# An RWKV block with sixteen routed experts: whole slots of 128 rows plus mixed slots of four 32-row pieces

## What is computed

```
x = x + attn(_layernorm(x))          # time mix (r, w, k, v, two scans, Wo), channel mix (Wkey, relu^2, Wval, gate Wrec)
x = x + ffn(_layernorm(x))
# ffn, t = 8192 tokens, 16 experts, top 1
logits = hidden @ router_w.T
top_vals, top_idx = top_k(logits, 1)
scores = sigmoid(...)                                   # zero for all experts but the chosen one
routed_in = hidden[None] * scores.T[:, :, None]
gate, up = split(einsum('nth,nhf->ntf', routed_in, gate_up_proj))      # 128 -> 2 x 128
routed = einsum('ntf,nfh->nth', up * silu(gate), down_proj).sum(0)     # 128 -> 128
shared = silu(hidden @ shared_gate.T) * (hidden @ shared_up.T) @ shared_down.T   # width 512
```

## Time and profile before

| | us |
|---|---|
| median of 3 runs | 490.42 |
| the profiled execution | 490.73 |
| its span, first to last instruction | 488.6 |
| granted TensorE clock, mean | 0.999 |
| PE busy in the span | 477.0 |
| DVE, ACT, POOL busy | 371.1, 323.8, 352.3 |
| transposes of the first two pairs start | 353.0 |
| last down product of a slot, end | 467 |
| last matmul, end | 483.9 |

### The profile page before, as it was taken

The page is one execution under the profiler, slowest core; times in us unless marked ns, Lnnn a source line. Parts: engine busy times, 40 slices in busy tenths (PEclk is TensorE's granted clock), DMA queues, the critical chain, the costliest instruction groups (busy, mean ns, idle before and its releaser), DMA issues.

```text
span 488.6 us, 10463 instructions
## 1 busy us (share of the span) xinstructions
PE 477.0 (98%) x3093; PEld 388.2 (79%) x3093; DVE 371.1 (76%) x1056; ACT 323.8 (66%) x623; POOL 352.3 (72%) x573
## 2 busy tenths in 40 slices
PE   8999999999999999999999999999999999999995
PEld 7655777868777778686777867888899999999995
DVE  7889899899999998997899989747445555555535
ACT  2667887978978879777687886554365555555521
POOL 6655688898888988986788777677236676667750
PEclk9999999999999999999999999999999999999999
DMA  7007001102101011020101101111389854442028
GB/s 238 2 1 281 22 12 56 54 13 66 33 34 65 24 45 54 12 67 21 46 25 41 45 1 44 45 44 37 117 197 225 226 158 136 145 139 76 24 52 294
DMA packets 33031, 39.33 MB, mean 80 GB/s; under 512 B 4913, under 2 KB 29113, under 8 KB 32720
## 3 DMA queue, kind: packets, MB, share of 16 engines
q1 hardware_dynamic: 26640, 24.98, 17.8%
q0 software_dynamic: 5760, 13.16, 7.8%
q10 hardware_dynamic: 576, 0.52, 0.3%
HBM read 21.69 MB, written 17.93 MB: 81 GB/s over the span
## 4 chain that ended last, share of the span: by engine, by line
PE 77%; DVE 6%; issue 5%; POOL 5%; DMA 4%; ACT 2%; SPq 1%; POOLq 0%; DVEq 0%; ACTq 0%
PE bank L427 17%; PE bank L420 9%; PE bank L444 6%; PE bank L414 4%; PE bank L822 3%; PE bank L823 3%; PE bank L815 3%; PE bank L435 3%; PE bank L528 3%; PE bank L514 3%; PE bank L540 3%; PE bank L524 3%; PE bank L519 3%; PE bank L688 2%; PE bank L697 2%
## 5 line engine op out<-in xcount | busy, mean ns | idle before, releaser
L427 PE MATMUL bank<-hT,wm 128*128 128x256 f32 x512 | 124.7, 383 | 0.6 <-ACT kr L908 0.6
L427 PEld LDWEIGHTS bank<-hT,wm 128*128 128x128 f32 x512 | 92.0, 190 | 18.7 <-issue 8.3
L1528 POOL DMA_INDIRECT sorted_rows<-rows,posi x64 | 71.9, 1124 | 19.6 <-issue 16.9
L1612 POOL DMA_INDIRECT out<-shared x55 | 53.2, 967 | 37.3 <-DVE shared L1442 22.3
L420 PEld LDWEIGHTS bank<-wm,k 128*128 128x128 f32 x512 | 61.7, 192 | 7.6 <-issue 6.6
L420 PE MATMUL bank<-wm,k 128*128 128x128 f32 x512 | 62.1, 275 | 0.0
L1084 ACT ACTIVATE er<-bank 128x256 f32<-128x256 f32 x40 | 15.4, 384 | 44.8 <-PE bank L823 44.3
L1450 DVE TENSOR_TENSOR e<-er,bank 128x256 f32<-128x256 f32 x40 | 16.9, 421 | 23.0 <-ACT er L1084 21.1
L444 PE MATMUL bank<-wm,actA 128*128 128x128 f32 x240 | 32.9, 280 | 0.0
L1612 POOL DMA_INDIRECT out<-rows x24 | 23.1, 964 | 11.3 <-DVE rows L1442 5.3
L944 ACT ACTIVATE h<-rows,smE 128x128 f32<-128x128 f32 x64 | 26.3, 482 | 6.7 <-POOL smE L1504 6.7
(11 more groups left out here) (256 smaller groups left out, 1293.9 us busy)
## 6 DMA issues: line engine op xcount, KB each, us to landing
shared<-sorted_rows SPq DMA_DIRECT2D x56, 128.5 KB, 2.9
shared<-x SPq DMA_DIRECT2D x16, 256.0 KB, 3.0
rows<-sorted_rows SPq DMA_DIRECT2D x24, 128.5 KB, 2.5
wexp<-w_exp SPq DMA_DIRECT2D x2, 1536.0 KB, 8.4
sorted_rows<-filler SPq DMA_DIRECT2D x17, 128.5 KB
shared<-out SPq DMA_DIRECT2D x6, 256.0 KB, 4.7
out<-shared SPq DMA_DIRECT2D x12, 128.0 KB, 2.7
sorted_rows<-rows,posi POOLq DMA_INDIRECT x64
```

Of the source, the lines that this page charges most:

```text
L427: ins = mm(dst[:, j * HALF:(j + 1) * HALF], W(name, 2 * pair_ + j), src[:, half * HALF:(half + 1) * HALF], start=True, stop=True)
L1528: g_.indirect_dma_start(sorted_ap, bass.IndirectOffsetOnAxis(posi[t % 3][:, g:g + 1].bitcast(U32), 0), rows[t % 3][:, g, :], None).then_in ...
L1612: g_.indirect_dma_start(out, bass.IndirectOffsetOnAxis(xr[k % RING][:, j, D:D + 1].bitcast(U32), 0), xr[k % RING][:, j, D + 1:ROW], None, ...
```

## The change

The slots are cut in another way. There are now 48 whole slots (`UNI`), always of one expert, and 20 mixed slots of four pieces of 32 rows (`SUBS` = 80 pieces), each piece with an expert of its own: 24 whole pairs and 10 mixed pairs, 34 in all. The pairs 5, 8, 11 and so on to 32 are the mixed ones. For a mixed slot SP issues four loads of 32 rows, ACT copies four sets of weights, and PE makes four gate and four up products with 32 columns of the transposed rows each, and four down products whose stationary operand has 32 columns and whose result goes to 32 partitions. The filler is 32 rows for an expert, and all 16 of its DMAs are issued in one go ahead of pair 5, with a wait for all of them. The ring of weight copies grows to 23, and ACT copies up to four pieces a turn ahead. The tables take 18 steps on DVE and their constants are made ahead of the third tile's `z` step.

```diff
-NS = NTOK // P + NE
-NP = NS // 2
+SUB = P // 4
+UNI = NTOK // P - NE
+SUBS = NTOK // SUB + NE - 4 * UNI
+NS = UNI + SUBS
+MIXED = range(5, 34, 3)
+NP = UNI // 2 + len(MIXED)
...
-        xw = [q, an, xn2T, th, rv]
-        XW = len(xw)
+        xw = q + an + xn2T + th + rv + k2 + a + xa + kr[2:4] + h
...
+        def parts(k):
+            return 4 if k in MIXED else 1
...
+        def copied(m):
+            return min(copies_to(NP - 1), max(copies_to(min(m, NP - 1)), 4 * (m + 1))) if m >= 0 else 0
...
             for k in range(NP):
-                if k in FILL_PAIRS:
-                    sp.dma_start(sorted_ap[bass.ds(tails[k - FILL_PAIRS[0]], P), :], filler[:, :]).then_inc(s["fill_out"], 16)
-                if k == FULL_SLOTS // 2:
+                if k == MIXED[0]:
+                    tails = entries(SP_ENGINE, tail_i, 0, FILL_ROW - P, NE)
+                    for row in tails:
+                        sp.dma_start(sorted_ap[bass.ds(row, SUB), :], filler[0:SUB, :]).then_inc(s["fill_out"], 16)
                     sp.wait_ge(s["fill_out"], 16 * (NE + 1))
                 for j in range(2):
-                    sp.dma_start(xr[k % RING][:, j, :], sorted_ap[bass.ds(first_rows[at_ + j], P), :]).then_inc(
-                        s[loaded(k)[0]], 16)
+                    if k in MIXED:
+                        for c in range(4):
+                            sp.dma_start(xr[k % RING][c * SUB:(c + 1) * SUB, j, :],
+                                         sorted_ap[bass.ds(sub_rows[entry(k, j, c) % LOADED], SUB), :]).then_inc(s[loaded(k)[0]], 16)
...
-                    for j in stores(k):
-                        ins = mm(grp(XDN_B[k % 2], j), grp(xact[k % 4], j), w_of(k, j, 2), start=True, stop=True)
+                    for j in range(2):
+                        for c in range(parts(k)):
+                            rows_ = slice(c * SUB, (c + 1) * SUB) if k in MIXED else slice(0, P)
+                            ins = mm(grp(XDN_B[k % 2], j)[rows_, :], grp(xact[k % 4], j)[:, rows_], w_of(k, j, c, 2),
+                                     start=True, stop=True)
-                    for j in stores(k):
-                        mm(grp(XGU_B[k % 2], j), w_of(k, j, 0), xhT(k, j), start=True, stop=True)
-                        ins = mm(grp(XGU_B[k % 2], 2 + j), w_of(k, j, 1), xhT(k, j), start=True, stop=True)
+                    for j in range(2):
+                        for c in range(parts(k)):
+                            rows_ = slice(c * SUB, (c + 1) * SUB) if k in MIXED else slice(0, P)
+                            mm(grp(XGU_B[k % 2], j)[:, rows_], w_of(k, j, c, 0), xhT(k, j)[:, rows_], start=True, stop=True)
+                            ins = mm(grp(XGU_B[k % 2], 2 + j)[:, rows_], w_of(k, j, c, 1), xhT(k, j)[:, rows_], start=True, stop=True)
...
+            def copy_weights(first, last):
+                for i in range(first, last):
+                    k, j, c = copy_of(i)
+                    if i >= len(xw):
+                        wait(act_e, "xDN", copy_of(i - len(xw))[0])
+                    af(xw[i % len(xw)][:, 0:EW], wexp[:, bass.ds(expert_of(words, entry(k, j, c)) * EW, EW)], ACT.Copy).then_inc(s["xw"], 1)
...
+                    if t == 2:
+                        table_consts()
```

More of the change, by code:

```diff
@@ L117, in wait, with grp @@
                 eng.wait_ge(s[name], (count - 1) * PER[name] + (PER[name] if k is None or t not in of else k))
+        def grp(tile, g):
+            return tile[:, g * P:(g + 1) * P]
         wm = sb("wm", MAIN_COLS)
@@ L168, in program @@
         oh = ring("oh", 2, (G, NE), BF16)
[L170 to L173, removed]
+        start_of = sb("start_of", (2, NE))
+        cnt_i, blocks_i, blocks, ahead = sb("cnt_i", (2, NE), I32), sb("blocks_i", (2, NE), I32), sb("blocks", (2, NE)), sb("ahead", NE)
+        cum, whole, rest, left = sb("cum", 1 + 2 * NE), sb("whole", NE + 1), sb("rest", NE), sb("left", NE)
+        step_of, sums, sum2 = sb("step_of", 2 * NE), sb("sums", (2, 2 * NE)), sb("sum2", 2)
+        is_sub, sub4, sub16, place_a, place_b, place_u = (sb(n, 1) for n in ("is_sub", "sub4", "sub16", "place_a", "place_b", "place_u"))
+        place16, place4 = (grp(xa[0], i).rearrange("p (w k) -> p w k", k=PACK) for i in range(2))
+        place = sb("place", WORDS)
         rowm, eidc = sb("rowm", 1), sb("eidc", 1)
@@ L322, in tl_sem @@
                 return "tl_in", 16 * (len(GP_LOADS) - 1)
-            return f"xr_in{u // 2}", 32 * laps(u // 2)
+            return loaded(max(range(u // 2, NP, RING)))
         def all_stored(eng):
@@ L802, in one_turn @@
                     wait(pe, "xhT", k // 2 - 1)
-                    for i in [i for i in range(4) if i % 2 in stores(k + i // 2)]:
+                    for i in range(4):
                         if i % 2 == 0:
@@ L1068, in _ @@
             wait(act_e, "e", NT)
+            wait(act_e, "hs", NT)
             for u, step in late_order()[1:STEPS_BEFORE]:
                 late_step(u, step)
-            def one_turn(m):
-                for k in pair(m, W_BEHIND):
-                    wait(act_e, "xDN", k - XW)
-                    for j in range(2):
-                        af(xw[k % XW][j][:, 0:EW], wexp[:, bass.ds(expert_of(words, 2 * k + j) * EW, EW)], ACT.Copy).then_inc(
-                            s["xw"], 1)
+            def copy_weights(first, last):
[4 more added lines that the diff above has]
+                    af(xw[i % len(xw)][:, 0:EW], wexp[:, bass.ds(expert_of(words, entry(k, j, c)) * EW, EW)], ACT.Copy).then_inc(s["xw"], 1)
+            def one_turn(m):
+                copy_weights(copied(m - 1), (copied(m - 1) + copied(m)) // 2)
                 if m < NP:
@@ L1170, in tables @@
[L1170 to L1174 removed]
+                tab(v.tensor_tensor(cnt_i[:, :, :], region[:, :].unsqueeze(1).to_broadcast([P, 2, NE]), start_of[:, :, :], ALU.subtract))
@@ new lines, in tables @@
+                tab(v.tensor_scalar(blocks_i[:, 0, :], cnt_i[:, 0, :], P.bit_length() - 1, None, ALU.logical_shift_right))
+                tab(v.tensor_scalar(blocks_i[:, 1, :], cnt_i[:, 1, :], SUB.bit_length() - 1, None, ALU.logical_shift_right))
+                tab(v.tensor_copy(blocks[:, :, :], blocks_i[:, :, :]))
+                tab(v.tensor_tensor_scan(ahead[:, :], one16[:, :], blocks[:, 0, :], 0.0, ALU.mult, ALU.add))
+                tab(v.tensor_scalar(cum[:, 1:1 + NE], ahead[:, :], float(UNI), None, ALU.min))
@@ new lines, in tables @@
+                tab(v.tensor_tensor(whole[:, 0:NE], cum[:, 1:1 + NE], cum[:, 0:NE], ALU.subtract))
+                tab(v.scalar_tensor_tensor(rest[:, :], whole[:, 0:NE], -4.0, blocks[:, 1, :], ALU.mult, ALU.add))
+                tab(v.tensor_tensor_scan(cum[:, 1 + NE:1 + 2 * NE], one16[:, :], rest[:, :], float(UNI), ALU.mult, ALU.add))
+                tab(v.tensor_scalar(left[:, :], blocks[:, 1, :], -1.0, float(REGION // SUB), ALU.mult, ALU.add))
+                tab(v.tensor_scalar(step_of[:, 0:NE], whole[:, 0:NE], -4.0, float(REGION // SUB), ALU.mult, ALU.add))
@@ new lines, in tables @@
+                tab(v.scalar_tensor_tensor(step_of[:, NE:2 * NE], whole[:, 1:1 + NE], 4.0, left[:, :], ALU.mult, ALU.add))
+                tab(v.scalar_tensor_tensor(place_u[:, :], whole[:, 0:1], sub4[:, 0:1], place_a[:, :], ALU.mult, ALU.add))
+                tab(v.tensor_scalar(sums[:, 0, :], cum[:, 1:1 + 2 * NE], slot_p[:, 0:1], None, ALU.is_le))
+                tab(v.scalar_tensor_tensor(sums[:, 1, :], cum[:, 1:1 + 2 * NE], slot_p[:, 0:1], step_of[:, :], ALU.is_le, ALU.mult))
+                tab(v.reduce_sum(sum2[:, :], sums[:, :, :], AX))
```

97 lines of the change are left out of this document (49 added, 48 removed).

## The result

The changed kernel takes 535.38 us (median of 4 runs, 528.12 to 539.53) beside 490.70 us of the kernel before; the ratio is 1.083, with a 95% interval of 1.071 to 1.095. The forecast was 525.0 in a range of 512 to 536: the sign and the range held, the value was 2% low. The four executions lie in the order of their granted clock (528.1 us at 0.982, 534.7 at 0.970, 536.1 at 0.965, 539.5 at 0.959). The ratio is taken from the two quicker of them, since the other two lie over 1.5% above the quickest.

A forecast was written before the change was run, and what follows sets the result against it. PE's passes, added up and paced by weight loads, were taken to bound the turns. 490.7 + 21.5 passes + 12.1 wait + 1.5 clock + 0.6 constants - 1.4 end = 525.0 us, range 512 to 536.

The forecast's parts named there:

- PE's passes: PE's turns: 48 whole slots 37.2 us plus 20 mixed 45.5, against 61.2 before, +21.5 us with nothing to hide it.
- wait of T in turn 4: PE's T pass waits for pair 5 behind SP's 16 fillers, their landing, a table read and eight loads: +12.1 us.
- clock behind the wait: PE standing at pair 5 loses its granted clock for a while: +1.5 us, between 0 and 4.
- constants: Ten small DVE steps ahead of the third tile's z, 2.4 us, partly fitting idle time: +0.6 us, from 0 to 2.4.
- end: After PE's last matmul, loaded rows are already there, so 3.3 us to span's end instead of 4.7: -1.4 us.
- The step that decided the case: Gate and up passes of mixed slots: a narrow pass is paced by its 128-column weight load, 0.111 us, gaining nothing.
- The down products: Mixed pairs' down products with 32 stationary columns, priced from the router's row: 0.78 us a pair, 0.39 a slot.
- Tables, ACT and POOL: Added table steps (about 1 us), 48 more ACT copies and fewer POOL scatters: nothing on the path while PE's wait lasts.
- Paced by columns: Rival on PE's narrow passes: they cost their moving columns, about 0.03 us each, time 499 us; chance 0.11.
- its share everywhere: Rival: 32-row DMA issues cost a quarter and narrow passes their columns, time 485 us; chance 0.05.
- short issues: Rival on SP: 32-row issues are short, saving 9.2 us, while passes stay load-paced, time 516 us; chance 0.10.
- load and columns added up: Rival on PE: a narrow pass costs its weight load plus its columns, +8.7 us, time 534 us; chance 0.12.

The follow-up runs named there:

- the execution of 527.38 us: One execution of the unchanged changed kernel, from its second series (median 529.23 us, ratio 1.081); its profile is the one read, granted clock 0.982.
- the first series: The changed kernel's first 4 runs against the kernel before: median 535.38 us, 528.12 to 539.53, ratio 1.083.
- the kernel with 128 columns: Changed kernel with each mixed-slot piece's gate and up products moving all 128 columns instead of 32: 524.82 us, ratio 1.069 to the kernel before.
- the kernel with one weight set: Changed kernel with fillers early, 128 columns moved, and only the first piece's gate and up products per mixed slot: 488.92 us, ratio 0.996.

## Why the prediction held, and where it was off

Step by step against the execution of 527.38 us; its span is 37.1 us longer than before, the forecast's terms came to 34.3.

| term | forecast | measured |
|---|---|---|
| PE's passes | +21.5 | +20.8, what the other rows leave |
| wait of T in turn 4 | +12.1 | +10.5 |
| clock behind the wait | +1.5 (0 to 4) | +2.1 |
| clock under the narrow passes | no term | +3.4 here, more in other executions |
| constants | +0.6 | +0.7 |
| end | -1.4 | -0.4 |

**Passes.** The step that decided the case held: a narrow pass costs what a wide one does, 0.111 us in the timeline and 0.1124 where 240 of them were left out. That it is the weight load that sets this price, and not some other cost of every pass, is argued and not shown, since no run changes the weights' columns alone. The down passes, with 32 weight columns, take 0.58 / 16 = 0.036 us each, which speaks for the load, but they also go to four groups of partitions. The Trainium skill's rule of columns plus a small gap, with its floor of about 25 ns (page "TensorE: Matmul & The Clock Gate", Back-to-back issue gap), by which I priced a rival, is given there for an isolated matmul; in a stream of weight loads and matmuls, the page says, both set the spacing. The trace speaks against the former: 0.111 us a pass with 32, 64 and 128 columns alike. The down products were put a little too high: 0.68 us a pair in place of 0.78, 1.0 us in all. The first two passes of a narrow run take 0.07 us less than two others, but the wide work behind the run takes as much longer:

```profile
486.95 1.19 PE L459 MATMUL bank<-wm,den 128*128 128x128 f32 x8
487.98 0.61 PE L841 MATMUL bank<-k,e 128*128 128x128 f32 x4
```

These eight passes, at the full clock behind a run of 32, take 1.03 us in place of 0.94. So the forecast's own count comes to about 20.5, and 0.3 us of the 20.8 is left without a place.

**The wait.** SP's steps came as written: ten loads, the table, 16 fillers at 0.53, eight loads. The third pass came 372.64 - 361.47 = 11.2 us later, 0.7 of it with the first load (350.49 in place of 349.82: the constants), 10.5 by the wait. Where the 1.6 us less lie is seen in the chain of work that ended last (start, length):

```profile
364.72 1.48 DMA sorted_rows<-filler
...
370.88 1.72 DMA shared<-sorted_rows
```

The last filler lands in 1.48 us and the last load in 1.72, where I had put 2.2 for each; the rest is issues and a table read that went slightly quicker.

**The clock** is the term that was mis-sized, because half of its cause was missing. Behind the wait it cost 7.4 x 0.29 = 2.1 us, within the bounds, and 2.2 in the kernel before with the same wait. But I reasoned that only a PE that stands loses its clock. Two falls behind mixed pairs (387 to 391 us, and a like one near 450) cost 1.7 us each in this execution; behind the other eight of its ten runs of narrow passes the clock stays full. How many such falls an execution has varies, and that makes the spread: the profile of the execution of 539.53 us has seven, which cost 15.3 us in place of 3.4, and 11.9 of the 12.2 us between the two executions are these. One of its windows, columns as above:

```profile
400.00:420.00 20.00, 20.00 (x139) 19.04 (x139) 6.89 (x14) 11.21 (x27) 8.69 (x9) 0.83 0.34 94
```

The median of the first series lies 10.4 us above the forecast. By its clock, about 0.967, this term comes to some 11 us there, an estimate (3.4 and 0.015 x 530), so it makes up the miss almost alone. The Trainium skill tells of clock lost to gaps in which PE stands (the same page, HAM oscillation). The wait here agrees, with 0.50 from 372 to 376 us; the falls at 387 us come while PE's row is busy 3.00 of 3.00 us, and no gap explains them.

**Constants** are put at the 0.7 us by which SP's first load came later; no run leaves them out. With the same work ahead of it that load came at 351.68 in the kernel with 128 columns, 1.9 us later than before, so the agreement with 0.6 may be chance. **Tables, ACT and POOL** at nothing held: in the turns PE waits for nothing but the 10.4 us above and 0.4 us for ACT, and ACT's and SP's added work cost nothing in the kernel with one weight set. **The end** hardly shortened: I had DVE find its rows loaded, yet at 518.37 it still waits for them, and at PE's last matmul it is still adding, so it is 0.4 us shorter and not 1.4.

**Rivals.** Paced by columns (499) and its share everywhere (485) fell with the pitch; short issues (516) with SP's 0.50 to 0.53 us; load and columns added up (534) is near the median, but by accident: 32, 64 and 128 columns have the same pitch. That the median still lies in the range, 0.6 us below its upper end, is luck in part: the range reached so far for the sake of this rival, and what filled it was a clock that the forecast did not have.

## What to carry to other kernels

Where f32 products of up to 128 moving columns follow each other without a gap, count weight sets, not columns: cutting a slot into four experts costs four times the passes and saves nothing. (Above 128 the columns count: eight passes of 256 take 1.73 us here, 443.20 to 444.93, in place of 0.94.) A burst of small DMAs ahead of loads that an engine needs soon costs its issue time whole, in an in-order queue; it belongs where the queue waits anyway, which gave back 7.8 us here. A busy PE row doesn't show that PE runs at full speed: read the granted clock in windows of a few us behind every unusual run, and if narrow products can't be avoided, put wide ones between them.

## What the runs showed of the hardware that I had not expected

- The granted clock fell to its lower level (0.50: 1.2 of 2.4 GHz) in the last 1.5 us of a run of 32 f32 passes with 32 moving columns each, or within 1 us behind it, with PE busy all the time. It did so at two of ten runs in the execution of 527.38 us and at seven of ten in that of 539.53 us. It stayed full with 64 or 128 columns, in runs of 8, and in runs of 16 with 128-column work between.
- At the lower level passes of every width go at about half speed: two of 32 columns took 0.42 us in place of 0.22 (387.05 to 387.47), the eight of 128 columns of L459 1.85 in place of 0.94, and the eight of 256 columns of L452 3.18 in place of 1.73.
- A DMA issue costs 0.50 to 0.53 us of SP's time with 32 rows and 0.52 with 128, but fillers of 32 rows had landed and let the next load go 2.3 us behind the last issue, those of 128 rows 6.0 us.
- Sixteen down passes with 32 weight columns each, to four groups of partitions, take 0.58 us and slow the two passes behind them by 0.1 us.
